# Graph network on one core: neighbour counts of two batches at a time, made once and kept in DRAM, for both plain sum rounds

## The reference

```
x = ln(x + rgcn16(x))   # layer 0: two rounds, mean per (target, relation), 16 relations
x = ln(x + gat(x))      # layer 1: attention, softmax over the edges of a target
x = ln(x + rgcn8(x))    # layer 2: sum over edges of x[src] @ W[type], 8 relations, batch norm
x = ln(x + sage(x))     # layer 3: two rounds
# one round of layer 3 ("plain sum round")
msg_sum = segment_sum(x[src], dst)
mean = msg_sum / max(degree, 1)
x' = mean @ W_l.T + b + x @ W_r.T
```

## Time and profile before

| | |
|---|---|
| median of three runs | 6337.98 us |
| the profiled execution | 6346.25 us, its span 6344.3 us |
| PE, busy share of the span | 71% |
| POOL | 70% |
| DVE | 44% |
| ACT | 30% |
| granted TensorE clock, mean | 0.842 of full speed |
| memory traffic | 447.41 MB read, 24.15 MB written |

### The profile page before, as it was taken

How to read it: one execution, slowest core, us unless ns; L and a number is a source line. 1 busy time by engine, 2 the same in 40 slices (tenths; PEclk the granted TensorE clock), 3 DMA queues, 4 the chain that set the end, 5 groups by cost and what they waited for, 6 DMA issues and landing times. The chain is left out here.

```text
span 6344.3 us, 119904 instructions
## 1 busy us (share of the span) xinstructions
PE 4533.7 (71%) x27080; PEld 3709.3 (58%) x27081; DVE 2761.6 (44%) x10683; ACT 1904.5 (30%) x4793; POOL 4416.5 (70%) x4559
## 2 busy tenths in 40 slices
PE   3488887878778886566666675565555888778886
PEld 3377777767777775455555555555554555555554
DVE  6643333333333332566666542222225554355543
ACT  0022222222222223444444441111114333243332
POOL 3067777757777773777777647777775777767777
PEclk6599999999999997566666688878887999989998
DMA  3066666642222211333333322111121222222222
GB/s 79 3 168 161 156 154 156 158 119 53 53 53 53 53 52 44 89 83 83 83 83 83 71 63 52 52 52 52 52 52 52 54 53 54 53 63 54 54 53 59
DMA packets 380915, 478.11 MB, mean 75 GB/s; under 512 B 123697, under 2 KB 293202, under 8 KB 380242
## 3 DMA queue, kind: packets, MB, share of 16 engines
q0 software_dynamic: 142336, 295.20, 18.3%
q1 hardware_dynamic: 233778, 174.99, 10.9%
q10 hardware_dynamic: 4128, 1.75, 0.1%
HBM read 447.41 MB, written 24.15 MB: 74 GB/s over the span
## 5 line engine op out<-in xcount | busy, mean ns | idle before, releaser
L1320 PE MATMUL PS<-ROOM 128*128 128x128 f32 x8320 | 1028.4, 282 | 130.6 <-ACT ROOM L942 130.6
L1320 PEld LDWEIGHTS PS<-ROOM 128*128 128x128 f32 x8320 | 972.9, 195 | 200.5 <-ACT ROOM L942 147.7
L942 ACT COPY ROOM<-PS 128x512 f32<-128x512 f32 x1040 | 609.7, 586 | 1390.5 <-PE PS L1330 1387.1
L777 POOL DMA_INDIRECT GB<-table,IDX x832 | 793.0, 953 | 316.6 <-issue 252.1
L747 POOL DMA_INDIRECT GB<-table,IDX x576 | 571.4, 992 | 217.5 <-issue 174.4
L1969 DVE TENSOR_TENSOR ROOM<-ROOM,PS 128x128 f32 x312 | 89.7, 288 | 1362.7 <-PE PS L1338 1359.0
L777 POOL DMA_INDIRECT GB<-in_x,IDX x416 | 402.8, 968 | 370.7 <-ACT IDX L923 234.0
L747 POOL DMA_INDIRECT ROOM<-table,IDX x544 | 519.1, 954 | 165.8 <-issue 164.9
L1330 PE MATMUL PS<-OH,GB 128*128 128x256 f32 (+1 forms) x1664 | 387.9, 403 | 314.4 <-DMA GB<-table,IDX 253.0
L1330 PEld LDWEIGHTS PS<-OH,GB 128*128 128x128 f32 x1664 | 326.4, 248 | 361.3 <-issue 288.2
L735 POOL DMA_INDIRECT GB<-table_gat,IDX x416 | 426.6, 1025 | 127.7 <-issue 124.2
(11 more groups left out here) (386 smaller groups left out, 8405.6 us busy)
## 6 DMA issues: line engine op xcount, KB each, us to landing
H<-one_over SPq DMA_DIRECT2D x416, 128.0 KB
ROOM<-one_over SPq DMA_DIRECT2D x416, 128.0 KB
ROOM<-local_row SPq DMA_DIRECT2D x104, 256.0 KB
GB<-table,IDX POOLq DMA_INDIRECT x1408
ROOM<-table,IDX POOLq DMA_INDIRECT x960
GB<-in_x,IDX POOLq DMA_INDIRECT x416
H<-in_x,IDX POOLq DMA_INDIRECT x416
H<-table,IDX POOLq DMA_INDIRECT x416
```

Source lines behind the costliest of these rows:

```text
L777: pool.indirect_dma_start(out=r.rows[c][:, j * P:(j + 1) * P], out_offset=None, in_=r.dram[:, :], in_offset=bass.IndirectOffsetOnAxis(ap=I ...
L942: act.copy(to.rearrange("p r (j d) -> p r j d", j=r.per), of.rearrange("p (j d r) -> p r j d", j=r.per, d=NEAR))\
L1320: ins = nc.tensor.matmul(PS[:, 4, 0:P], r.near[1 - b][:, t * P:(t + 1) * P], r.weights[:, t * P:(t + 1) * P], start=t == 0, stop=t == r.re ...
```

## The change

- A dense unit is now two batches, 16 tiles, in one window of 128 target nodes. Of every four batches (`CYCLE`) the first two are a dense unit and the other two are sparse: 26 units and 52 sparse batches a round. The last, ungrouped batches of a round go.
- The counts are built once, during the round of layer 2: in three of every four steps of `near_round(near_c)` five, five and six tiles are built (`TILES_OF`), each with a one-hot of 600 columns instead of 800 (12 targets a tile for 16). PE builds in one pair of PSUM banks. ACT takes the counts out to `MADE_UP` at the tile's own offset in the window, with the first column of each block set aside in `SIDE`, and DVE adds that column (`correct`), because neighbouring tiles may share a node. SP writes each finished unit to a DRAM tensor (128 x 6800 bf16).
- In both plain sum rounds SP loads a unit's counts from DRAM to `NEIGH[e]` when the unit two before has been applied, and PE waits for the load. `build`, `take_out` and the one-hots L2326 and L2327 leave these rounds.
- The eight one-hots of a sparse batch, and the eight of a batch in the round of layer 2, are made by one TENSOR_TENSOR comparison of 128x1024 each.
- Ahead of the round of layer 2 DVE computes for each unit whether its tiles fit (gaps of 1 to 11 nodes between tiles, at most 128 nodes in all), its first node and its tile offsets, and clears `MADE_UP`; two small DMAs spread a row of them.
- Buffers move: `REST_X` to `OH`, with four buffers for six, `OHR` and `bn` into shared room, `BASIS` and `MIXED` swap places.

Cut to its core:

```
+CYCLE = 4
+DENSE = BATCHES // CYCLE
+SPARSE = BATCHES - 2 * DENSE
+TILES_OF = (range(0), range(0, 5), range(5, 10), range(10, 16))
...
 # SP
+            with sp.Fori(0, DENSE) as d:
+                sp.wait_ge(mx_cor, d * PAIR + PAIR)
+                sp.dma_start(neighbours[bass.ds(d, 1), :, :]..., MADE_UP).then_inc(made_out, 16)
+            def load(m, d, e):
+                if not isinstance(d, int) or m.d0 + d >= 2:
+                    sp.wait_ge(mx_app, d + (m.d0 - 1))
+                sp.dma_start(NEIGH[e]..., neighbours[bass.ds(d, 1), :, :]...).then_inc(mx_ld[e], 16)
...
 # ACT, in the round of layer 2
+            def take_out(d, n, j, offsets):
+                t = d * PAIR + j
+                if j == 0:
+                        act.wait_ge(made_out, d * 16)
+                if n == 0 and (not isinstance(t, int) or t > 0):
+                    act.wait_ge(mx_cor, t)
+                ...
+                act.wait_ge(mx_built, t + 1)
+                if j == 0:
+                    act.copy(MADE_HALVES[:, :, :, 0:SPAN], counted_of(2)).then_inc(mx_out, 1)
+                else:
+                    act.copy(MADE_HALVES[:, :, :, bass.ds(offsets[n] + 1, SPAN - 1)], counted_of(2)[:, :, :, 1:SPAN])
+                    act.copy(SIDE[:, n, :]..., counted_of(2)[:, :, :, 0]).then_inc(mx_out, 1)
...
 # PE, in the round of layer 2: tiles 0 and 1 of a step ahead of its gathered rows, 2 and 3 after unit 0, the rest after unit 1
+            def count_tile(d, n, j):
+                t = d * PAIR + j
+                pe.wait_ge(mx_hot, t + 1)
+                if not isinstance(t, int) or t > 0:
+                    pe.wait_ge(mx_out, t)
+                for a in range(2):
+                    ins = nc.tensor.matmul(PS[:, 2 + a, 0:KEYS // 2], HOT_LO[:, n, :], HOT_KEY[n][:, ...], start=True, stop=True)
+                ins.then_inc(mx_built, 1)
...
 # DVE, end of each step of the round of layer 2
+                    if counting and now < BATCHES:
+                        mine, later = TILES_OF[c], TILES_OF[(c + 1) % FOUR]
+                        if mine:
+                            offsets = offsets_of(dve, i, mine)
+                            dve.wait_ge(mx_out, i * PAIR + (mine[-1] + 1))
+                        if later:
+                            hot_tiles(i, later, range(2))
+                        if mine:
+                            correct(i, mine, offsets)
+                        if later:
+                            hot_tiles(i, later, range(2, len(later)))
...
 # DVE, one-hots of a sparse batch
-                    for j in range(part * G // 2, (part + 1) * G // 2):
-                        ins = dve.tensor_scalar(oh(b, j), iota_f[:, :], local[:, bass.ds(n + j, 1)], None, ALU.is_equal)
+                    dve.tensor_tensor(OH[:, b, :].rearrange("p (j n) -> p j n", j=G), mid(iota_f[:, :], G),
+                                      last(local[:, bass.ds(n, G)], P), ALU.is_equal).then_inc(mx_oh, 1)
 # and in the round of layer 2
+                    if not r.weighted:
+                        dve.tensor_tensor(r.hot[b]..., mid(iota_w[:, 0:r.cols], G), last(r.key[:, bass.ds(k * G, G)], r.cols), ALU.is_equal).then_inc(near_hot, 1)
+                        return
...
 # PE, plain sum round
+                    if half == 0:
+                        pe.wait_ge(mx_ld[e], i * 16 + 16 * (m.d0 // 2 + 1))
-                        if not isinstance(d, int) or d < DENSE - 1:
-                            for j in tiles_of(w):
-                                build(d + 1, j)
```

More of the change, by code:

```diff
@@ L567, in tile_first, with dense_first, offsets_of @@
             return values[0]
-        def batch_of(i, c):
[L571 to L577, removed]
+        def dense_first(engine, d, kk, j):
+            _, values = nc.values_load_multi_w_load_instructions(
+                meta[:, :, :].rearrange("o k m -> o (k m)")[0:1, bass.ds((d * CYCLE + kk) * META + (j + (4 + G)), 1)],
+                engines=[engine.engine], min_val=0, max_val=NODES - 1)
+            return values[0]
+        def offsets_of(engine, d, tiles):
+            first = [j for j in tiles if j < G]
+            second = [j - G for j in tiles if j >= G]
+            found = []
+            for kk, js in ((0, first), (1, second)):
+                if js:
+                    found += meta_of(engine, d * CYCLE + (2 + kk), 4 + G + js[0], len(js), LATEST)
+            return found
+        def batch_of(i, c):
+            return 2 * CYCLE * i + (CYCLE * (c // 2) + 2 + c % 2)
         block = ctx.enter_context(nc.Block())
@@ L870, in step @@
[L870 to L874, removed]
+                def step(i, c):
+                    g = RING * i + c
+                    if not isinstance(g, int) or g + 3 < SPARSE:
+                        act.wait_ge(mx_sum, g * G + (m.g0 * G + TWO))
+                        stage(i + (c + 3) // RING, (c + 3) % RING)
+                    if not isinstance(g, int) or g < XBLOCKS:
@@ L934, in step @@
                         act.copy(MADE[1 - b][:, :], PS[:, 4, 0:P]).then_inc(made_sb, 1)
+                    tiles = TILES_OF[c] if counting and now < BATCHES else range(0)
+                    if tiles:
+                        offsets = offsets_of(act, i, tiles)
+                        for n in range(2):
+                            take_out(i, n, tiles[n], offsets)
                     if now < BATCHES:
@@ L943, in step @@
                                 .then_inc(near_sb, 1)
+                            if tiles:
+                                for at in range(2 + 2 * n, 4 if n == 0 else len(tiles)):
+                                    take_out(i, at, tiles[at], offsets)
                     if now < BATCHES - FOUR:
@@ L1322, in step @@
                         ins.then_inc(made_ps, 1)
+                    tiles = TILES_OF[c] if counting and now < BATCHES else range(0)
+                    if tiles:
+                        for n in range(2):
+                            count_tile(i, n, tiles[n])
                     if now < BATCHES:
@@ L1332, in step @@
                             ins.then_inc(near_ps, 1)
+                            if tiles:
+                                for at in range(2 + 2 * n, 4 if n == 0 else len(tiles)):
+                                    count_tile(i, at, tiles[at])
                     if 1 <= now <= BATCHES:
@@ L1562, in done @@
                             pe.sem_inc(g_passed, 1)
-                        for q in range(G):
+                        for q in range(FINE):
                             done(11 + 2 * q)
```

467 lines of the change are left out of this document (247 added, 220 removed).

## The result

The kernel after takes 6452.2 us (median of 4 runs, 6440.9 to 6459.2) against 6340.6 us, a ratio of 1.0176 [1.0161, 1.0191]. I forecast 6135 us, in 6005 to 6275, with 0.06 for slower. Its profiled execution took 6447.5 us at a span of 6445.7, so 101.4 us more span than before. My sum was 202.6 us less: an error of 304 us.

A forecast was written before the change was run, and what follows sets the result against it. POOL's gathers were taken to bound layer 2's and the plain sum rounds: profiled 6346.3 - 362.6 (gathers) + 49 (comparisons) + 111 (counting) = 6143.7 us; the profiled execution lies 8.3 above the median, so 6135 us, range 6005 to 6275.

The forecast's parts named there:

- The bound before: Layer 2's and plain sum rounds: POOL's gathers run without a stop, 1.257 us each, and set both rounds' end.
- the gathers removed: Plain sum rounds: 144 gathers fewer in each, so a round loses 181.3 us and both lose 362.6 us.
- The rest of a plain sum round keeps up: Plain sum rounds: PE needs 425 us of some 545 and stays hidden; loads of the counts cost nothing.
- Rival C: Plain sum rounds: loads of the counts set the pace, 6473 us at 40 us a load; chance 0.05.
- One comparison for eight: Plain sum rounds: each 128x1024 comparison on DVE holds POOL's gathers for 0.47 us, +49 us (0 to 114).
- the 11.24 us gather: Start of the plain sum round: one long gather beside DVE's subtractions, taken to stay as it is.
- Counting inside layer 2's round, the chain's side: Layer 2's round: the counting chain takes 44.5 us per four batches, above POOL's 42.7, and sets the pace: +111 us.
- DVE's tail: Layer 2's counting steps: after the last take-out DVE makes one-hot and keys and corrects five columns, 3.25 us.
- The last piece: Layer 2's round, unit's end: the next first take-out waits for the write to DRAM, put at 10.5 us.
- The step without tiles: Layer 2's round, the step that builds no tiles: needs 6.0 us and lies beside the write.
- B: Layer 2's round: counting chain longer by hand-overs and register loads, 49 us per four batches, 6253 us; chance 0.20.
- The end of the round: Between layer 2's last gather and the first plain gather: last write and first loads fit the 55 us, costing nothing.

The follow-up runs named there:

- e4: Kernel after with both 128x1024 comparisons undone, eight short TENSOR_SCALARs again in layer 2's and both plain sum rounds: 6328.8 us, ratio 0.9986 to the kernel before.
- e6: Kernel after without VectorE's wide-batch branch in layer 2's loop, eight short comparisons, constants for DVE's and ACT's offset loads (wrong result): 5987.2 us, 0.9450 of before.
- e9: Kernel after without VectorE's wide-batch branch, eight short comparisons, DVE's offset loads moved ahead of its wait for PE's placed rows: 6155.6 us, 0.9712 of before.
- e1: Kernel after without VectorE's never-taken wide-batch branch in layer 2's loop, body 216 instructions instead of 377: 6351.6 us, ratio 1.0021 to the kernel before.
- e10: Kernel after without wide-batch branch, eight short comparisons, DVE's and ACT's offset loads earlier, 16 side columns taking corrections off the chain: 5975.6 us, 0.9427 of before.

## Why the prediction was wrong, step by step

**The bound before, and the gathers removed: right.** 416 gathers a round; POOL's pace held.

**The rest of a plain sum round keeps up: right.** POOL waits for nothing there; the 1700 KB loads at 131 GB/s in all, 0.41 of the DMA engines, are hidden. Rival C fell.

**One comparison for eight: right in mechanism, 42 us for 49.** I held the 11.24 us gather of the earlier trace rows to stay. It is gone: the longest gather of the plain sum rounds after is 1.98 us, and in e4, without comparisons, 1.26. (The second round before had such a gather too, of 11.19 us.) That is the larger part of the 12 us by which each plain sum round of e4 (522.0) lies below my 534.2, and with the 7 us of the comparisons most of the 32 us by which the two rounds came out shorter than my sum. The subtractions now come in pairs of 1.25 us, and the gathers beside them start every 1.25 us too.

**Counting inside layer 2's round, the chain's side: this step failed.** Its pieces:

| piece | put at | after, the pass above | after, mean of 25 passes | e6 (no loads), mean |
|---|---|---|---|---|
| five tiles, first to last take-out, first step | 7.9 | | 8.3 | 7.5 |
| from the last take-out to the next step's first (DVE's tail), first step | 3.25 | 6.4 (4224.69 to 4231.05, next pass) | 6.2 | 3.6 |
| five tiles, second step | 7.9 | | 8.2 | 6.8 |
| DVE's tail, second step | 3.25 | 7.4 (4181.64 to 4189.05) | 7.3 | 4.2 |
| six tiles | 9.55 | 9.2 (4189.05 to 4198.25) | 9.8 | 8.8 |
| last take-out to last correction | 2.1 | 6.15 (4198.25 to 4204.40) | 6.3 | 2.8 |
| last correction to the next unit's first take-out | 10.5 | 11.8 (4204.40 to 4216.18) | 11.5 | 7.0 |
| the pass | 44.5 | | 57.6 | 40.6 |

The tiles, with all the hand-overs between PE and ACT that I was unsure of, were nearly right: 1.0 us too little for the three steps together. So the lower clock isn't the main cause either, as PE's counts lie in these pieces. DVE's tail was wrong: it left out the register loads, 2.5 to 3.3 us before each step's work, for which I had put "about 0.3 for waits, registers, hand-over" beside ACT's tiles and nothing at all on DVE; and a correction takes 0.49 us, not 0.35. By the means the three excesses, 3.0, 4.0 and 4.2, make 11.2 of the 13.2 us by which a pass is longer than my 44.5. In e6, without the loads, the same three pieces take 3.6, 4.2 and 2.8 us, near what I had put. The loads are worth 11.3 us a pass in e6, with ACT's gone as well, and 5.2 in e9, with DVE's moved alone.

The last piece came out near my figure by luck. The write lands in 6.3 us, not 10.5, nearer to the 4.9 us that I had estimated from the Trainium skill ("SBUF — State Buffer", its summary table); what filled the time is the code fetch of 8.24 us on DVE, of which I had no thought. Without it, in e1, the piece takes 6.9 us. The step without tiles, which I had "beside the write", begins with DVE's one-hots, and DVE was still waiting for its code. That such stalls exist could be read before: in near_a's round, whose body has 373 instructions, the trace of the kernel before has DVE idle for 9.75 us and waiting for no one (48 instruction transfers between 600 and 1000 us; no run tested this loop):

```profile
679.86 0.48 DVE L1880 SCALAR_TENSOR_TENSOR H<-iota_w,key,ROOM 128x256 f32<-128x256 f32 x1 [9.75 <-issue]
```

Of the rivals, B said this (a longer chain by hand-overs and register loads), but at 49 us for four batches. I had worked its price out from nothing that a row showed.

**The end of the round: put at 0, measured +36 us.** POOL gathers up to four batches ahead, so the last three counting steps lie wholly behind the last gather. In e10, with the chain short, the gap is 58.4 us, 3.4 above before.

## What to carry to other kernels

Before work is laid into a stage with room, list for each engine on the new chain everything between its waits, the register loads too, and place those where the engine already waits: here the place of five or six loads a step was worth 5 us a pass on one engine; without them on either it was 11. A loop's body that grows has a price of its own where the chain passes through that engine: count its instructions, with the branches that are never taken, against loops of the same kernel that show idle time at their head. And of two forms of an operation on an engine that isn't the bound, take the one that leaves the bound alone, though it be the slower.

## Not expected of the hardware

- Loading five column offsets into registers held DVE for 2.5 us where they lie together (2.2 in e1) and for 3.0 us where they come from two places, six for 3.27 us (ACT 2.7 to 2.9 us). The Trainium skill ("Runtime: NRT & Kernel Launch", Instruction fetch mechanics) gives some 0.2 us a register for loads from HBM, an estimated 1.2 us for six; here, from SBUF and with the instructions that go with each, six come to 0.55 us each.
- VectorE fetched a loop body of 373 to 377 instructions again in each pass, 4 to 5 transfers a pass, for a stall of 4 to 8.6 us (4.6 to 5.1 us with bodies of 433 and 435); with bodies of 216, 272 and 305 instructions there was hardly a transfer. In the profile it is idle time "issue" or "DVEq" once a pass, and transfers in the queue named instruction.
- A write of 1700 KB from SBUF to DRAM landed 6.3 us after its issue, 276 GB/s.
